# Filled strips of heads, value matmuls of four tiles at once, and two closing steps behind the pieces

## The reference

```python
x = x + causal_attention(layernorm(x))            # 16 query heads of 128, one key/value head, rotary
x = x + cross_attention(layernorm(x), ctx, mask)  # 16 heads of 16, ctx is 1500 x 256 a sequence
x = x + ffn(layernorm(x))                         # both inputs rounded to 8 bits, gate * silu
```

```python
scores = clip(q @ k.T / 4, -50, 50);  scores = where(mask, scores, -50)
probs  = softmax(scores);             ctx = probs @ v
delta  = layernorm(clip(rs, 0, 0.3) * (ctx @ Wo.T + bo)) * gamma + beta
```

## Time and profile before

| what | value |
|---|---|
| median of three runs | 1442.66 us (1442.17 to 1444.83) |
| the profiled execution | 1444.34 us, its span 1442.4 us |
| TensorE busy | 1376.7 us, 95% of the span |
| VectorE busy | 1013.8 us, 70% |
| ScalarE busy | 716.9 us, 50% |
| GpSimd busy | 447.3 us, 31% |
| the two blocks | `block_a` to about 375 us, `block_b` from there |

### The profile page before, as it was taken

The page is one execution under the profiler, slowest core; times in us unless marked ns, Lnnn a source line. Parts: engine busy times, 40 slices in busy tenths (PEclk is TensorE's granted clock), DMA queues, the critical chain, the costliest instruction groups (busy, mean ns, idle before and its releaser), DMA issues.

```text
span 1442.4 us, 54968 instructions
## 1 busy us (share of the span) xinstructions
PE 1376.7 (95%) x25094; PEld 1176.8 (82%) x25094; DVE 1013.8 (70%) x1792; ACT 716.9 (50%) x939; POOL 447.3 (31%) x400
## 2 busy tenths in 40 slices
PE   5899999998899999999999999999999999999983
PEld 5687787786688888888888888888888888888872
DVE  4676676666136787786777777687878778677765
ACT  3445445444255645555555555555554555555540
POOL 4332333222222333333324233233333333332400
PEclk9999999999899999999999999999999999999995
DMA  9100001000111121111112121111212121121100
GB/s 260 23 1 31 1 1 31 1 30 1 58 49 57 31 77 44 56 58 46 58 37 63 31 77 52 57 49 45 64 31 77 41 62 55 45 61 34 49 2 7
DMA packets 38808, 66.75 MB, mean 46 GB/s; under 512 B 3605, under 2 KB 36818, under 8 KB 38578
## 3 DMA queue, kind: packets, MB, share of 16 engines
q1 hardware_dynamic: 38578, 63.24, 15.1%
HBM read 61.40 MB, written 1.84 MB: 44 GB/s over the span
## 4 chain that ended last, share of the span: by engine, by line
PE 71%; DVE 2%; issue 0%; POOL 0%; POOLq 0%; DVEq 0%
PE proj_ps L1277 19%; PE proj_ps L1268 19%; PE score_ps L1295 14%; PE sum_ps L1315 12%; PE side_ps L1350 2%; PE side_ps L1332 2%; PE side_ps L1364 1%; PE side_ps L1357 1%; PE side_ps L1339 0%; DVE inv L1109 0%; DVE exps L1097 0%; DVE amax L1150 0%; DVE hidden L1182 0%; DVE hidden L1193 0%; DVE sig L1192 0%
## 5 line engine op out<-in xcount | busy, mean ns | idle before, releaser
L1049 ACT ACTIVATE exps<-score_ps 125x1792 f32<-125x1792 f32 x192 | 320.5, 1669 | 419.0 <-PE score_ps L1295 419.0
L1097 DVE TENSOR_SCALAR exps<-exps,top 125x896 f32<-125x896 f32 x384 | 287.9, 791 | 18.0 <-ACT exps L1049 17.5
L1295 PE MATMUL score_ps<-spread,keys 32*125 32x112 f32 x6144 | 219.3, 279 | 0.0
L1315 PEld LDWEIGHTS sum_ps<-exps,vals 125*32 125x32 f32 x12288 | 163.0, 110 | 50.9 <-issue 34.4
L1088 DVE COPY vals<-proj_ps 125x512 f32<-125x512 f32 x192 | 128.2, 687 | 103.4 <-PE proj_ps L1277 103.0
L1295 PEld LDWEIGHTS score_ps<-spread,keys 32*125 32x125 f32 x6144 | 185.1, 183 | 15.4 <-issue 0.4
L1315 PE MATMUL sum_ps<-exps,vals 125*32 125x56 f32 x12288 | 191.5, 214 | 2.9 <-DVE exps L1097 2.9
L992 POOL TENSOR_TENSOR low<-raw_early,high 128x500 fp32r<-128x500 f32 x64 | 100.8, 1583 | 231.2 <-issue 115.4
L992 POOL TENSOR_TENSOR low_early<-raw_early,high_early 128x500 fp32r<-128x500 f32 x62 | 104.3, 1691 | 172.3 <-issue 104.1
L1041 ACT ACTIVATE keys<-proj_ps,b_k 128x500 f32<-128x500 f32 x192 | 129.9, 677 | 52.4 <-PE proj_ps L1268 52.4
L286 POOL TENSOR_TENSOR swapped<-swapped,sin 128x448 f32<-128x448 f32 (+1 forms) x72 | 88.6, 1232 | 138.5 <-ACT swapped L507 138.5
(11 more groups left out here) (156 smaller groups left out, 2411.6 us busy)
## 6 DMA issues: line engine op xcount, KB each, us to landing
raw_early<-in_ctxT SPq DMA_DIRECT2D x64, 500.0 KB, 4.0
raw<-in_ctxT SPq DMA_DIRECT2D x32, 500.0 KB, 3.5
w_q<-in_attn_Wq SPq DMA_DIRECT2D x4, 512.0 KB, 8.1
w_o<-in_attn_Wo SPq DMA_DIRECT2D x1, 2048.0 KB, 21.5
out<-y_out SPq DMA_DIRECT2D x16, 112.0 KB, 1.9
rows<-in_x SPq DMA_DIRECT2D x1, 1344.0 KB, 16.8
raw_early<-in_ffn_gate_wT SPq DMA_DIRECT2D x1, 1024.0 KB, 9.6
raw_early<-in_ffn_val_wT SPq DMA_DIRECT2D x1, 1024.0 KB, 5.1
```

Source lines behind the costliest of these rows:

```text
L1049: nc.scalar.activation(exps[t % 2][:, :, :, :].rearrange("p h r n -> p r h n"), score_ps[0:TILE, :, 0:2 * QW].rearrange("p r (h n) -> p r ...
L1097: nc.vector.tensor_scalar(tile, tile, LIMIT_LO, top[:, n, at:at + 1], ALU.max, ALU.min)\
L1295: ins = nc.tensor.matmul(score_ps[0:TILE, r, to:to + HE * S], keys[c % 2][32 * r:32 * r + 32, k, (at + half) * TILE:(at + half + 1) * TILE ...
L1315: ins = nc.tensor.matmul(sum_ps[32 * h:32 * h + VW, g, :], vals[c % 2][:, at + half, HJ * g + h, :], exps[t % 2][:, half, r, col:col + S], ...
```

## The change

- `value_and_ones` (new): for heads of odd groups the 32 columns are taken 16 columns earlier, so they are the ones before the head and then its values. Totals then lie in the first 16 rows of a strip and values in the last 16. Even groups stay as they are.
- `read_sums` is four instructions on half the width. With the two columns of `part` (1 and 0 by row) they put the values of an even and an odd group together into `sums`, and the totals of both into `totals`. Both are 128 x 2 x 56, with all rows filled. `sums_read` is counted up by a separate instruction behind them.
- `divide` shuffles the totals first (now a swap of the two halves of a strip), then takes one reciprocal for both kinds of groups, multiplies and adds the bias, all on 112 columns where there were 224.
- `project` is two matmuls where there were four, and `w_xo` and `b_v` are laid out anew on the host; their loads at the start are three where there were eight (with the new `part`).
- `add_up` is called on even steps alone, for the tiles of two steps one behind the other: 64 matmuls in a row. `exps` has three buffers where there were two. In the last pair the last two calls stand alone.
- `AFTER = (2, 5)`: `project` and `turn_rows` stand behind the two pieces of their step on TensorE. On VectorE the step 5 copy of the turned rows stands between the two value copies; `project` at step 2 stays where it is, since an even step has no such copies.

```diff
--- before
+++ after
@@ -45,7 +45,8 @@
 SP = 64
 RING = 3
 TOTALS = (3, 7, 11)
-N_EARLY = 11 + 2 * HJ
+N_EARLY = 14
+WEIGHTS_AT = 13
 
 TILE = 125
 CHUNK = 500
@@ -58,7 +59,10 @@
 NT = PT // 2
 BN = BT // 2
 GATES = (7, 8)
-SWAP = [HD + n % HD for n in range(2 * HD)]
+AFTER = (2, 5)
+SWAP = [(n + HD) % (2 * HD) for n in range(2 * HD)]
+READS = 4
+DIVS = 7
 VW = 2 * HD
 
 ROUND = 12582912.0
@@ -784,8 +788,9 @@
         self.mask_i = sb("mask_i", [TILE, BATCH, BT], I32)
         self.top = sb("top", [TILE, BATCH, BT])
         self.ident_h = sb("ident_h", [P, P], BF16)
-        self.b_v = sb("b_v", [P, HG])
-        self.w_xo = sb("w_xo", [P, HG, D])
+        self.b_v = sb("b_v", [P, HG // 2])
+        self.w_xo = sb("w_xo", [P, HG // 2, D])
+        self.part = sb("part", [P, 2])
         self.b_xo = sb("b_xo", [ROWS, D])
         self.res = sb("res", [ROWS, 1])
         self.ln_gamma = sb("ln_gamma", [ROWS, D])
@@ -809,11 +814,8 @@
                  (self.gate_b[:, :], dram["ffn_gate_b"].partition_broadcast(ROWS)),
                  (self.val_b[:, :], dram["ffn_val_b"].partition_broadcast(ROWS)),
                  (self.out_b[:, :], dram["ffn_out_b"].partition_broadcast(ROWS))]
-        for j in range(HJ):
-
-            pairs += [(self.b_v[32 * j:32 * j + HD, :], dram["xattn_bv"][j]),
-                      (self.w_xo[32 * j:32 * j + HD, :, :],
-                       dram["xattn_WoT"].rearrange("(a j d) n -> j d a n", a=HG, j=HJ)[j])]
+        pairs += [(self.b_v[:, :], dram["xattn_bv"]), (self.part[:, :], dram["c_part"]),
+                  (self.w_xo[:, :, :], dram["xattn_WoT"].rearrange("(a p) n -> p a n", p=P))]
         assert len(pairs) == N_EARLY
         return pairs
 
@@ -870,16 +872,17 @@
         high = [early.high, sb("high1", [P, DC, CHUNK], F32R)]
         low = [early.low, sb("low1", [P, DC, CHUNK], F32R)]
         w_h, w_l, b_k, spread, top = early.w_h, early.w_l, early.b_k, early.spread, early.top
-        head_of, ident_h, b_v, w_xo, b_xo, res = early.head_of, early.ident_h, early.b_v, early.w_xo, early.b_xo, early.res
+        head_of, ident_h, b_v, w_xo, b_xo, res, part = (early.head_of, early.ident_h, early.b_v, early.w_xo,
+                                                              early.b_xo, early.res, early.part)
         ln_gamma, ln_beta, gate_b, val_b, out_b = early.ln_gamma, early.ln_beta, early.gate_b, early.val_b, early.out_b
         keys = [sb(f"keys{n}", [P, DC, CHUNK]) for n in range(2)]
         vals = [sb(f"vals{n}", [TILE, CT, XH, VW]) for n in range(2)]
 
-        exps = [sb(f"exps{n}", [TILE, 2, HR, QW]) for n in range(2)]
-
-        sums = sb("sums_b", [P, 2, HG, S])
-        inv = sb("inv", [P, 2, HG, S])
-        heads = sb("heads", [P, HG, 2, S])
+        exps = [sb(f"exps{n}", [TILE, 2, HR, QW]) for n in range(3)]
+
+        sums = sb("sums_b", [P, 2, HG // 2, S])
+        totals = sb("totals", [P, 2, HG // 2, S])
+        heads = sb("heads", [P, HG // 2, 2, S])
         delta = sb("delta", [ROWS, D])
         x3 = sb("x3", [ROWS, D])
         z3 = sb("z3", [ROWS, D])
@@ -1045,8 +1047,8 @@
 
                 act.wait_ge(scores_ready, NT * i + t + 1)
                 if warm:
-                    act.wait_ge(probs_used, NT * i + t - 1)
-                nc.scalar.activation(exps[t % 2][:, :, :, :].rearrange("p h r n -> p r h n"),
+                    act.wait_ge(probs_used, NT * i + t - 2)
+                nc.scalar.activation(exps[t % 3][:, :, :, :].rearrange("p h r n -> p r h n"),
                                      score_ps[0:TILE, :, 0:2 * QW].rearrange("p r (h n) -> p r h n", h=2),
                                      ACT.Exp, scale=0.25).then_inc(exps_ready, 1)
 
@@ -1059,7 +1061,7 @@
                 for t in range(NT):
                     c, half = divmod(t, 2)
                     x = PC * i + c
-                    exp_twin(i, t, not first or t >= 2)
+                    exp_twin(i, t, not first or t >= 3)
                     if half == 0:
                         for p in range(DC):
                             if not (last and c == PC - 1):
@@ -1092,27 +1094,35 @@
             def limit(i, t, half):
 
                 dve.wait_ge(exps_ready, NT * i + t + 1)
-                tile = exps[t % 2][:, half, :, :].rearrange("p r n -> p (r n)")
+                tile = exps[t % 3][:, half, :, :].rearrange("p r n -> p (r n)")
                 n, at = 2 * i + t // BN, 2 * (t % BN) + half
                 nc.vector.tensor_scalar(tile, tile, LIMIT_LO, top[:, n, at:at + 1], ALU.max, ALU.min)\
                   .then_inc(probs_ready, 1)
 
             def read_sums(i, k):
 
+                even, odd = sum_ps[:, 0::2, :], sum_ps[:, 1::2, :]
+                chain = Chain(dve, div_step, DIVS * (2 * i + k))
                 dve.wait_ge(probs_used, NT * i + BN * (k + 1))
-                nc.vector.tensor_copy(sums[:, k, :, :], sum_ps[:, :, :]).then_inc(sums_read, 1)
+                chain.inc(nc.vector.tensor_scalar(totals[:, k, :, :], odd, part[:, 0:1], None, ALU.mult))
+                chain(nc.vector.tensor_scalar(sums[:, k, :, :], odd, part[:, 1:2], None, ALU.mult))
+                chain.inc(nc.vector.scalar_tensor_tensor(totals[:, k, :, :], even, part[:, 1:2], totals[:, k, :, :],
+                                                         ALU.mult, ALU.add))
+                chain(nc.vector.scalar_tensor_tensor(sums[:, k, :, :], even, part[:, 0:1], sums[:, k, :, :],
+                                                     ALU.mult, ALU.add))
+                nc.vector.sem_inc(sums_read, 1)
+                assert chain.n == READS
 
             def divide(p, k):
 
-                dve.wait_ge(sums_read, 2 * p + k + 1)
-                chain = Chain(dve, div_step, 6 * p + 3 * k)
-                chain(nc.vector.reciprocal(inv[:, k, :, :], sums[:, k, :, :]))
-                nc.vector.sem_inc(inv_ready, 1)
-                chain(nc.vector.stream_shuffle(inv[:, k, :, :].rearrange("p a s -> p (a s)"),
-                                               inv[:, k, :, :].rearrange("p a s -> p (a s)"), SWAP))
-                chain(nc.vector.tensor_tensor(heads[:, :, k, :], sums[:, k, :, :], inv[:, k, :, :], ALU.mult))
-                nc.vector.tensor_tensor(heads[:, :, k, :], heads[:, :, k, :],
-                                        b_v[:, :].unsqueeze(2).to_broadcast([P, HG, S]), ALU.add)\
+                chain = Chain(dve, div_step, DIVS * (2 * p + k) + READS)
+                chain(nc.vector.stream_shuffle(totals[:, k, :, :].rearrange("p a s -> p (a s)"),
+                                               totals[:, k, :, :].rearrange("p a s -> p (a s)"), SWAP))
+                chain(nc.vector.reciprocal(totals[:, k, :, :], totals[:, k, :, :]))
+                chain(nc.vector.tensor_tensor(sums[:, k, :, :], sums[:, k, :, :], totals[:, k, :, :], ALU.mult))
+                assert READS + chain.n == DIVS
+                nc.vector.tensor_tensor(heads[:, :, k, :], sums[:, k, :, :],
+                                        b_v[:, :].unsqueeze(2).to_broadcast([P, HG // 2, S]), ALU.add)\
                   .then_inc(heads_ready, 1)
 
             def side(p, n):
@@ -1228,13 +1238,16 @@
                         read_sums(i - 1, 1)
                     if t == BN + 1:
                         read_sums(i, 0)
-                    if t in tail:
+                    if t in tail and t not in AFTER:
                         tail[t]()
                     if last and t == BN + 3:
                         divide(i, 0)
-                    if half == 1 and not (last and c == PC - 1):
-                        for q in range(2):
-                            values_copy(PC * i + c + 1, q, (c + 1) % 2)
+                    for q in range(2) if half == 1 and not (last and c == PC - 1) else ():
+                        if q == 1 and t in tail and t in AFTER:
+                            tail[t]()
+                        values_copy(PC * i + c + 1, q, (c + 1) % 2)
+                    if half == 0 and t in tail and t in AFTER:
+                        tail[t]()
                 if not first:
                     tail[NT]()
 
@@ -1299,6 +1312,11 @@
                                 start=True, stop=True)
                 ins.then_inc(scores_ready, 1)
 
+            def value_and_ones(r, tile, head):
+
+                at = (tile * XH + head) * VW - (HD if head // HJ % 2 else 0)
+                return vals[r][:, :, :, :].rearrange("p t h v -> p (t h v)")[:, at:at + VW]
+
             def add_up(i, t, warm):
 
                 c, at = t // 2, 2 * (t % 2)
@@ -1313,8 +1331,8 @@
                             k, r, e = (HJ * g + h) // (HR * HE), (HJ * g + h) // HE % HR, h % HE
                             col = (k * HE + e) * S
                             ins = nc.tensor.matmul(
-                                sum_ps[32 * h:32 * h + VW, g, :], vals[c % 2][:, at + half, HJ * g + h, :],
-                                exps[t % 2][:, half, r, col:col + S],
```

(27 more changed lines are left out.)

## The result

The changed kernel takes 1433.9 us (median of four runs, 1429.7 to 1436.2), the kernel before 1443.6 beside it: a ratio of 0.9931, interval 0.9911 to 0.9950. The direction was right and the size was not. 9.7 us were gained of 28.7 forecast, and 1433.9 lies above the range's upper end of 1429.

The account below looks back on a forecast made before the run. TensorE's time was taken to bound the dense stretch. Merge 13.0, `project` 12.8 and the end 3.1, less 0.2 for stalls, gave 28.7 us saved and a forecast of 1414.3 us, range 1407 to 1429.

Parts of the forecast that it names:

- What bounds the kernel: From 400 to 1340 us only time on TensorE counts; other engines count only where they would now come late.
- Merge: Two `add_up` in a row on TensorE save 0.14 us for each of 95 calls, 13.0 us; bounds 0 and 23.
- The seam: Between two `add_up` in a row on TensorE: taken as free, the second costing 0.78 us where a lone one costs 0.92.
- The rule on drains: Skill rule for TensorE: changing the tiling mode drains the array, a change of tile within a mode does not; no price.
- Project: `project` on half the matmuls: 0.86 us saved in each of 15 closings inside the dense stretch, 12.8 us.
- Reads and divisions: On VectorE, hidden in the dense stretch: a divide falls from 3.0 us to about 2.0, the read takes 0.8 more.
- So no new stall, and 0.2 us of cost for all of them together: VectorE stays in time for the value copies, with about 0.8 to 0.9 us left at steps 1, 3 and 9.
- The end: From 1390.5 us, where VectorE leads: two divides, a read and `project` together save 3.1 us; bounds 2 and 4.
- The seam rival: Second `add_up` costs 0.92 us, waiting for its own semaphores and masked tiles; the merge brings 0; 1427 us, chance 0.13.
- the slower one through late copies: VectorE late for the value copies at steps 1, 3, 9: 1.2 us of stall each, 54 us; 1468 us, chance 0.05.
- The last one: Change doesn't do what it says: TensorE still alternates or `project` takes as long on two matmuls; near 1430, chance 0.03.

Follow-up runs that it names:

- 63 merges: Changed kernel with single value matmuls in 32 of 95 cycles, those whose scores would start at places 224 to 42 of a 256-instruction block; 1420.9 us, 0.9820.
- the 1430.4 of the same group of runs: Changed kernel with single value matmuls and `project` and `turn_rows` ahead of the pieces again (`AFTER` empty), filled strips kept; 1430.4 us, 0.9893.
- the second: Profile of the changed kernel run once more, unchanged, beside its variants on one chip; 1435.9 us, 0.9929 against the kernel before.
- the one with small loads: Changed kernel with context loads of 50 columns instead of 500 after the first three; 1428.8 us, 0.9897.

## Why the prediction was wrong

**What bounds the kernel.** Right that only TensorE's time counts, wrong in what its time can consist of. I asked which engine could be late for TensorE and checked ScalarE, VectorE and GpSimd. Its own instruction supply was in the page (the 3.24 MB of the instruction queue, 50,000 instructions in 1442 us), and I never set its rate against the burst that I lengthened.

**Merge.** The term itself is right. The seam is free: 1.71 us for 128 records where 0.92 + 0.78 = 1.70 was forecast, and undisturbed pairs take 62.42 us, with 64.08 - 6 x 0.136 - 0.86 = 62.40 expected. With all stops gone, 63 merges bring 7.6 us (1428.5 to 1420.9), or 9.5 against the 1430.4 of the same group of runs: 0.12 to 0.15 each. The rule on drains (the Trainium skill, TensorEngine Tiling (Array Packing), Key Properties) agrees with the seam.

**Project.** Right: 0.86 us for four records. With the merge undone the kernel gains 15.7 us on its neighbour (1444.2 to 1428.5); 12.8 for `project` and 3.1 at the end were forecast, 15.9.

**Reads and divisions.** Reciprocal 0.853 us, multiplications 0.275, fused reads 0.33, as worked out. The plain scalings out of PSUM take 0.32 to 0.33, not 0.27. All hidden, as said.

```profile
L1121 DVE RECIPROCAL totals<-totals 128x112 f32<-128x112 f32 x26 | 22.2, 853 | 0.9
L1107 DVE TENSOR_SCALAR totals<-sum_ps,part 128x112 f32<-128x112 f32 x25 | 8.2, 328 | 23.3 <-PE sum_ps L1333 23.3
L1122 DVE TENSOR_TENSOR sums_b<-sums_b,totals 128x112 f32<-128x112 f32 x26 | 7.2, 275 | 0.9
```

**"So no new stall, and 0.2 us of cost for all of them together".** This is the step that failed: the sum had 0.2 us for stalls of every kind, because only other engines were looked at. For VectorE it holds, TensorE never waits for the copies. But new stalls there are, 13.3 us in the first profile and 15.9 in the second over 14 pairs, and 2.4 in the last pair of the first. The profiled execution adds up. Saved without the stops: 23.2 in 14 pairs (14 x 1.66), 1.6 in the first, 0.6 in the last up to step 9, and 3.1 from there to the end, 28.6 in all, and 28.7 were forecast. An earlier start, which is chance, gives 1.9 more. Lost to the stops: 13.3, 0.4 in the first pair and 2.4 in the last, 16.0. That leaves 14.4, and the span is 14.4 to 14.5 shorter. The median lies 4.2 us above this execution, within what starts and stops vary by.

**The end.** From the scores of step 9 of the last pair to the end it took 53.61 us and takes 50.47: 3.14, forecast 3.1. In order of time: the last read of the sums 1.2 us, a divide 1.97, `project` 2.06.

**The rivals.** None had this mechanism. The seam rival (1427) and the slower one through late copies both name waits on semaphores, and there are none. The last one ("near 1430", 0.03) has the nearest number, but not the cause: the change does all that it says. The range was closed on the upper side by costs of work that I could see, and nothing in it stood for a resource whose state the profile of before did not show.

**What stays open.** The blocks' times explain where the stops are and, through the start of each transfer, how long they are. What stays open is why a transfer starts late where loads are in flight (1.5 to 2.7 us at the stops of step 1, 0.9 to 1.2 at most others); no experiment moved it but the one with small loads. Nor does a run show why the clock falls behind some stops of 1.8 to 2.5 us and not behind others. That a lone `add_up` (192 instructions with its scores) is safe is seen in 15 pairs at many places: there no block was begun less than 2.5 us after its landing, with 1.2 to 1.6 at the stops. With other work around it that margin would be another.

## What to carry to other kernels

When a change puts short instructions side by side on an engine that was dense, count instructions a microsecond over the burst, against the blocks in which they arrive: here 320 instructions in 2.8 us were too many where they began about 300 ahead of a block's first instruction, and 192 in 2.0 never were. What counts is the time for these last 300: 2.35 to 4.1 us where TensorE stopped, and 4.0 us or more in the kernels that have no stop and no added waits in their pairs. The sign of it is an engine that stops in the middle of a group with "issue" as its reason, always at the same places of the program. Then merge only where the place allows it: the same change gave 0.9929 merged everywhere, 0.9892 merged nowhere and 0.9820 merged by place.

## What the runs showed of the hardware that I had not expected

- TensorE's instructions come in blocks of 16 KB, 256 instructions. It never began a block less than 1.2 us after its transfer had landed (2456 blocks), and all 201 stops end 1.2 to 1.6 us after it. The transfer takes 0.9 to 1.5 us at the stops, and starts with some 300 instructions left to the block's first. Stops are mostly 0.3 to 1.6 us, up to 2.5 where loads are in flight.
- Behind four stops of 1.8 to 2.5 us the granted clock was 0.50 for 3.4 us, and the value pieces there took 4.3 to 4.6 us in place of 3.03.
- A wait that is met already costs TensorE about 0.10 us when many stand in a row (4.2 to 5.4 us for 42 to 52 of them, 0.2 without). 22 ahead of the first piece cost 1.5 us: from the last matmul before them to that piece 4.8 us where it is 3.2 to 3.3.
- On VectorE a multiplication and an addition of 0.39 us took 1.26 and 1.32 in the kernel with the merge alone, at the place where the order of the engines had shifted.
